# A graph network's scatter: one-hot rows made by GpSimd and VectorE together

## What is computed

```python
# first block: two relational layers
xt = einsum('nd,rde->rne', x, W)
agg = segment_sum(xt[rel, src], dst, num_segments=N)
x = relu(agg + x @ SW + b)
# second block: attention over the edges, softmax over the edges of one target
scores = (q[src] * k[tgt]).sum(-1) / 4 + curv @ Wc + bc
probs = exp(scores - smax[tgt]) / ssum[tgt]
messages = (probs[:, :, None] * v[tgt]).reshape(E, -1)
out = zeros_like(x).at[src].add(messages)
x = x + (out @ Wo + bo)
x = x + relu(layernorm(x) @ W1 + b1) @ W2 + b2
```

## Time and profile before

| | before |
|---|---|
| median of 3 runs | 9071.17 us (9058.99 to 9072.06) |
| span of the profiled execution | 9059.0 us |
| time of that execution | 9058.99 us, the shortest of the three |
| busy: PE, PEld | 6437.7 us (71%), 5123.3 us (57%) |
| busy: DVE, ACT, POOL | 5894.2 us (65%), 2567.4 us (28%), 6592.5 us (73%) |
| moved by DMA | 926.16 MB, mean 102 GB/s |

### The profile page before, as it was taken

How to read it: one execution, slowest core, us unless ns; L and a number is a source line. 1 busy time by engine, 2 the same in 40 slices (tenths; PEclk the granted TensorE clock), 3 DMA queues, 4 the chain that set the end, 5 groups by cost and what they waited for, 6 DMA issues and landing times. The chain is left out here.

```text
span 9059.0 us, 172600 instructions
## 1 busy us (share of the span) xinstructions
PE 6437.7 (71%) x29604; PEld 5123.3 (57%) x29605; DVE 5894.2 (65%) x18020; ACT 2567.4 (28%) x6875; POOL 6592.5 (73%) x6759
## 2 busy tenths in 40 slices
PE   6555555555688888888788888888745666666657
PEld 4443333333455555555588888887635555555555
DVE  4444444444566666666688888888845666666667
ACT  3111111111011111111355555555433333333322
POOL 6777777777777777777677777777667777777752
PEclk7556666666555555555555555555556777777778
DMA  5222222222222222222355555555435665666653
GB/s 196 60 64 64 64 64 64 65 64 62 52 61 62 62 62 62 62 62 62 96 136 137 136 136 136 136 137 136 121 78 129 152 150 144 155 150 149 149 135 78
DMA packets 1031683, 926.16 MB, mean 102 GB/s; under 512 B 210913, under 2 KB 911477, under 8 KB 1031495
## 3 DMA queue, kind: packets, MB, share of 16 engines
q0 software_dynamic: 214496, 443.25, 17.7%
q1 hardware_dynamic: 627671, 341.67, 14.8%
q10 hardware_dynamic: 189400, 139.98, 7.5%
HBM read 734.34 MB, written 192.49 MB: 102 GB/s over the span
## 5 line engine op out<-in xcount | busy, mean ns | idle before, releaser
L597 PE MATMUL stage_ps_agg<-stage_hot,stage_msg 128*128 128x128 f32 x6656 | 1562.7, 409 | 1349.4 <-DMA stage_msg<-xt,stage_index 1004.4
L597 PEld LDWEIGHTS stage_ps_agg<-stage_hot,stage_msg 128*128 128x128 f32 x6656 | 1355.4, 302 | 1632.4 <-issue 624.3
L1613 POOL DMA_INDIRECT slots<-big,stage_index x1664 | 1656.3, 995 | 512.5 <-issue 449.9
L586 POOL DMA_INDIRECT stage_msg<-xt,stage_index x1664 | 1624.6, 976 | 530.0 <-issue 472.3
L1157 POOL DMA_INDIRECT big<-q,stage_index x1664 | 1594.4, 958 | 546.9 <-issue 490.2
L586 POOL DMA_INDIRECT stage_msg<-xt_next,stage_index x1664 | 1601.9, 963 | 531.1 <-issue 513.7
L621 DVE TENSOR_TENSOR big<-big,stage_ps_agg 128x128 f32 x3328 | 952.6, 286 | 1432.0 <-PE stage_ps_agg L597 1072.2
L575 ACT ACTIVATE stage_index<-big 128x4 int32 (+1 forms) x832 | 170.2, 205 | 3698.9 <-PE stage_ps_agg L597 3655.7
L1656 PE MATMUL stage_ps_val<-nodes_a,big 128*128 x3328 | 665.6, 362 | 506.1 <-ACT big L1576 481.7
L1656 PEld LDWEIGHTS stage_ps_val<-nodes_a,big 128*128 128x128 f32 x3328 | 566.2, 257 | 549.8 <-issue 544.5
L1666 PE MATMUL stage_ps_sums<-stage_hot,big 128*128 128x128 f32 x4160 | 737.1, 343 | 107.5 <-DVE big L1784 101.4
(11 more groups left out here) (302 smaller groups left out, 9639.0 us busy)
## 6 DMA issues: line engine op xcount, KB each, us to landing
big<-slots SPq DMA_DIRECT2D x1976, 66.0 KB
big<-in_edge_attr_dram SPq DMA_DIRECT2D x1664, 64.0 KB
stage_trow<-targets ACTq DMA_DIRECT2D x830, 128.0 KB
stage_msg<-xt,stage_index POOLq DMA_INDIRECT x1664
stage_msg<-xt_next,stage_index POOLq DMA_INDIRECT x1664
big<-q,stage_index POOLq DMA_INDIRECT x1664
slots<-big,stage_index POOLq DMA_INDIRECT x1664
xt_next<-stage_xo SPq DMA_DIRECT2D x98, 256.0 KB, 2.9
```

What stands on the lines that cost most here:

```text
L586: pool.indirect_dma_start(self.msg[q][:, j, :], None, self.xt, bass.IndirectOffsetOnAxis(ap=self.index[q][:, j:j + 1], axis=0))\
L597: last = self.nc.tensor.matmul(self.ps[h][:, j, :], self.msg[q][:, j, :], self.hot[h][:, j, :], start=True, stop=True)
L1613: pool.indirect_dma_start(d["slots"], bass.IndirectOffsetOnAxis(ap=index[q][:, j:j + 1], axis=0), total[q][:, j, :], None).then_inc(s_sc[q ...
```

## The change

In the last part, of the five tiles of one-hot rows, GpSimd makes the first three (`BY_POOL`) with one compare each, `iota` with one column of `place`, and VectorE makes the other two with one compare of 128 x 2 x 128. GpSimd does so in a loop of its own behind its wait for the landed rows: it waits for the places (`s_place`), makes three tiles, and counts up a new semaphore, `c_pool_hot`. TensorE waits for that as well, from step 420 on. Before step 420 VectorE makes all five as before.

```diff
-    turns, SHARE, BY_SP = GP // SLOTS, 3, 2
+    turns, SHARE, BY_SP, BY_POOL = GP // SLOTS, 3, 2, 3
+    s_pool_hot = m.sem("c_pool_hot")
...
     def _(pool):
...
         for q in range(SLOTS):
             pool.wait_ge(s_sc[q], TURNS * 16 * G + at[q])
 
+        pool.addr_align(256, max_nops=1)
+        with pool.Fori(0, turns) as i:
+            for q in range(SLOTS):
+                y = i * SLOTS + (q + (PARTS - 1) * GP)
+                h = q % 2
+                ring_index(pool, s_place, y + 1, passed)
+                for j in range(BY_POOL):
+                    last = pool.tensor_scalar(hot[h][:, j, :], t["iota"][:, :], place[h][:, j:j + 1], None, ALU.is_equal)
+                last.then_inc(s_pool_hot, 1)
+
     @block.tensor
...
                 pe.wait_ge(s_hot, x.at() + (1 - FIRST))
+                if not x.within(0, FIRST, GROUPS + LAG):
+                    pe.wait_ge(s_pool_hot, x.at() + (1 - LAG - GROUPS))
...
     def _(v):
...
                 h, q = x.slot(1, 2), x.slot(1)
+                by_pool = 0 if x.within(1, FIRST, GROUPS + LAG) else BY_POOL
...
-                nc.vector.tensor_tensor(hot[h][:, :, :], t["iota"][:, :].unsqueeze(1).to_broadcast([P, SET, P]),
-                                        place[h][:, :].unsqueeze(2).to_broadcast([P, SET, P]), ALU.is_equal)\
+                nc.vector.tensor_tensor(hot[h][:, by_pool:SET, :],
+                                        t["iota"][:, :].unsqueeze(1).to_broadcast([P, SET - by_pool, P]),
+                                        place[h][:, by_pool:SET].unsqueeze(2).to_broadcast([P, SET - by_pool, P]),
+                                        ALU.is_equal)\
                     .then_inc(s_hot, 1)
```

## The result

The changed kernel is slower: 9106.65 us (median of 6, 9100.07 to 9113.06) beside 9072.08 us, ratio 1.0035 with a 95% interval of 1.0025 to 1.0045. In a second set of runs on one chip it was 9096.33 beside 9071.0, 1.0030 (1.0019 to 1.0042). The forecast was no change.

The account below looks back on a forecast made before the run. SyncE's issuing was taken to bound the last part at 2.509 us a step. Tail -0.4 to -0.7, semaphore +0.06 and 0 for the 52 steps took the median from 9071.2 to 9070.7 us, range 9053 to 9092.

Parts of the forecast that it names:

- The bound: Scatter's last part: SyncE's issuing of row loads sets the step at 2.509 us, VectorE alone would need about 2.38.
- (1): Last part: VectorE's compare shrinks from 825 to 420 ns, 21 us in 52 steps, none of which reaches the end.
- (2): Last part: GpSimd's three compares take 0.30 to 0.35 us each, hidden with 0.5 to 0.85 us to spare.
- the rival: Last part: GpSimd's compares and waits outlast a step, deciding from 0.63 us a compare; chance 4 in 100.
- The cover behind it: Last part: TensorE's products may start some 0.9 us later before VectorE's next place is late.
- (3): Last part: a held VectorE or GpSimd operation waits for one instruction of the other; cost nothing in the middle case.
- (4): Stage's end: one more semaphore to clear, +0.06 us; TensorE's waits and GpSimd's loop branches stand beside other work.
- All that the change can touch is 137 of 9059 us, 1.5%.: Whole kernel: the change acts only on the scatter's last part, from 8784 to 8921 us.
- (5): Last step to the stage's end: the chain after the last place gets shorter, -0.4 to -0.7 us.
- GpSimd being too slow: Last part: rival with GpSimd's compares outlasting a step, 9092 us, at the farthest 9149; chance 4 in 100.
- turns at the port: Last part: rival with VectorE waiting until all three GpSimd compares are over, 9117 or 9094 us; chance 5 in 100.
- VectorE is the bound after all: Last part: rival in which each step loses its 0.40 us, 20.8 us in all, 9050 us; chance 4 in 100.

Follow-up runs that it names:

- e7: Kernel before with SyncE issuing two and ScalarE three of a step's five loads in the last part: 9073.5 us, ratio 0.9999.
- e11: Kernel before with SyncE and ScalarE issuing three and two of the last part's five loads by turns: 9060.9 us, ratio 0.9987.
- c1: The kernel before, unchanged, run and profiled once more on the chip of the other runs of the set: 9071.0 us, ratio 1.000.
- e12: Changed kernel with SyncE and ScalarE issuing three and two of the last part's five loads by turns: 9092.6 us, ratio 1.0020.
- e6: Changed kernel with one of the five tiles on GpSimd instead of three: 9099.44 us, ratio 1.0031.
- e3: Kernel before plus a single unneeded GpSimd compare at the end of GpSimd's work in the scatter: 9094.01 us, ratio 1.0022.
- e4: Kernel before plus a single unneeded GpSimd compare at the start of GpSimd's work in the stage behind the scatter: 9097.1 us, ratio 1.0026.
- e9: Kernel before plus one GpSimd tensor_scalar subtraction at the start of GpSimd's work in the last stage: 9099.88 us, ratio 1.0025.
- c2: The changed kernel, run once more on the same chip as the others of the set: 9096.33 us, ratio 1.0030.
- e1: Changed kernel with GpSimd's loop keeping waits and increments but no compares, VectorE making all five tiles: 9074.69 us, ratio 1.0005.
- e2: Changed kernel plus a drain of GpSimd's queue between its wait for the landed rows and its loop: 9094.45 us, ratio 1.0027.

## Why the prediction was wrong, and where it was right

**The bound (right).** SyncE's issuing sets the step of 2.51 us: shown by e7 (the queue with three loads has it, whichever it is) and e11 (with neither at three the stretch is 5.8 us shorter than in c1).

**(1) VectorE's compare (right).** 425 ns for 420, and the relief of 21 us is idle time; with the queues out of the way it still doesn't arrive (e12). That the adds wait for the register load shows in the trace as well. In the median of the 52 steps the load (590 ns) starts 0.11 us after the compare and the first add 0.22 us after the load's end, in before, after, e11 and e12 alike, within 0.035 us in 51 steps of each. Meanwhile the compare's end moved from 0.13 us behind the load's end to 0.27 us ahead of it. So it isn't quite the load that ended last in before, as the forecast had it, but the load with the 0.22 us behind it.

**(2) GpSimd's compare (mis-sized, without effect).** 0.30 to 0.35 us was taken with 0.45 as the upper end; the second and third of a step take 0.60 us, one that meets nothing 0.62, the first of a step 0.73. A one-input row of another kind and a two-input row were no bounds for it. At 0.60 it stands just under the 0.63 from which the rival decided. The margin is gone: the third is ready 2.07 us after the places' end (8839.73 to 8841.80 in the timeline of after), when 2.1 was the limit, and TensorE waits for GpSimd in 8 steps, 24.1 us with the 17.4 us before the first one. The cover behind it, 0.9 us, took up these waits, for the last part isn't longer: 129.5 us in e12, where GpSimd makes three tiles, and 130.8 in e11, where it makes none.

**(3) Sharing (right).** VectorE's compare goes first and is never held, 425 ns; GpSimd's first is held until VectorE's is over. What the page of the Trainium skill says on it (SBUF — State Buffer, section Who interferes with whom), that the later of the two is blocked until the first is over, agrees with the trace of e6 in the order and nearly in the time. GpSimd's compare starts 0.17 us behind VectorE's and is finished 0.47 us after it, where its own 0.62 us behind the end of VectorE's would be a full block; 0.15 us of it go on beside VectorE's.

**(4) The semaphore and the rest (failed, some 5 us).** "The waits on TensorE's queue and the loop's branches on GpSimd's stand beside other work." What was moved was costed by what it runs beside; what comes behind it on GpSimd's queue wasn't looked at. There stood the drain of 8.56 us, in the trace of before as plainly as in that of after. Starting at 8780.5, it was hidden by the last part; behind a loop that ends 0.3 us before TensorE's last products begin, 5.0 us of it are not. With GpSimd's last compare forecast for 8917.4 the sum would have read 8917.4 + 8.56 = 8925.96, 4.7 us behind the last add of 8921.29. With the 0.2 us from a drain's end to the first clear that is 4.8 to 4.9 us, where the clears had begun 0.4 to 0.5 us behind the add: some 4.4 us.

**The term that was missing (the step that failed, 23 to 28 us).** "All that the change can touch is 137 of 9059 us, 1.5%." The sum starts from the span of before and changes only the last part and the clears; whatever lies ahead of 8784 us was put at nothing, because the change acts on that stretch alone. But the instructions ahead of it don't last as long as before: the 1664 DMAs of the scatter take 11 ns more by the median, 14 to 17 ns by the mean, because GpSimd's program has a kind of instruction more (e3, e4, e9). That is 23 us (c1 and c2) to 27.5 us in the length of the part. The length ran from 2161 to 2168 us in six executions without a new kind, and from 2180 to 2202 in eleven with one. 23 + 5 is 28 us, where the two sets of times give 25 and 35.

**(5) The tail (wrong, small).** It should have become 0.4 to 0.7 us shorter. It didn't: from the last place to the start of the last adds it is 4.42 us in both (8948.58 to 8953.00 in after). The adds of the step before start 1.02 us after the place in both, though the compare ends at 8949.19:

```profile
8948.77 0.42 DVE L1783 TENSOR_TENSOR stage_hot<-iota,stage_place 128x256 f32<-128x256 f32 x1
8949.60 1.15 DVE L1800 TENSOR_TENSOR big<-big,stage_ps_sums 128x128 f32 x5 [0.40 <-issue]
```

In the earlier trace rows the compare's end and the adds' start fall together, and that was read as one releasing the other ("here no register load covers it"). The load is there too: in before it runs from 8915.93 to 8916.52, in after from 8948.79 to 8949.38, and the first add follows its end by 0.22 us in both. The first of two things that end together must be told from the second before one of them is shortened.

**The rivals.** "Slower" had 8 in 100, by GpSimd being too slow or by turns at the port. Both decide from figures that were not reached; the loss came by neither. "VectorE is the bound after all" had 4 in 100 and fell in e12: with no queue in the way the 0.40 us a step are idle time all the same.

## What to carry to other kernels

Before work goes to an engine that idles, read what stands behind its last instruction, to the barrier: a drain or a clear that nobody sees today is paid once the engine ends last. Where an engine's program gets its first instruction of a kind, look afterwards at the shortest duration of those that were there, above all of one that runs 1664 times on the path; a test of one such instruction in a corner costs one run and would have told of 20 us ahead of the work. And when two queues share a job of five, let them take three by turns, for a fixed three sets the pace: here 5.8 us in the last part.

## What the runs showed of the hardware

- One tensor_scalar (0.62 us) in GpSimd's program, at the end of the scatter or in the stage behind it, raised the shortest of the scatter's indirect DMAs from 954 to 965 ns and the whole kernel by 0.22 to 0.26%, even where it ran after all of them. One tensor_copy raised the median of the gathers from 944 to 952 ns and that of the writes from 958 to 967. 156 tensor_tensor instructions of a kind that was there left both as they were. Even an affine select of the first microseconds (line 202) took 282 to 286 ns in ten executions with a tensor_scalar in the program and 287 to 289 in seven without. The cause within GpSimd wasn't shown.
- The first drain of GpSimd's queue behind 1664 indirect DMAs takes 8.56 us (8562 ns in each of the nine executions where no compare or subtraction stood ahead of it), counted from its last other instruction, however long ago the DMAs landed: some 135 us in e1, 0.2 us in the kernel before. A second one takes nothing of its own (e2). It isn't special to this stage: in the kernel before, the drains of both layers and of the score end 8.55 to 8.57 us after the end of the last gather, while the one of combine, which issues no indirect DMA, takes 0.04 us.
- GpSimd's compare with a column, 128x128 in float32, takes 0.60 us, more than its subtraction of the same column spread out as a second tensor, 0.39 us.
- A register load of three words takes 0.67 us on SyncE and 0.71 us on ScalarE, of two words 0.48 and 0.49 us.
